# PE's order within a step of a language-model tower: the transposed scores behind the side product

## The chip, the cores and the metric

The kernel runs on one core of one Trainium2 chip. The metric is device time in microseconds (us), the median of several runs. Shown are three runs of the kernel before: 5783.61 us in the median, 5773.73 to 5789.76.

## The reference

One layer of a language model on 16 rows of 1024 token ids. Each row goes through three parts with residual sums between them, and a layer norm ahead of the second and the third:

- the **token part**: embedding rows are gathered, multiplied by a matrix, taken through six gated convolutions (width 3, 128 to 256 channels), and multiplied by a second matrix;
- the **attention**: eight heads of 16 channels, with two softmax maps each (from Wq1, Wk1 and Wq2, Wk2). Statistics of both maps over windows of four rows feed a small gate network, which mixes the two maps;
- the **experts**: layer norm, a matrix, then one of eight two-layer networks (128 to 512 to 128, gelu), a last matrix and a gelu.

```python
attn1 = jax.nn.softmax(jnp.einsum('bhqd,bhkd->bhqk', q1, k1) * scale, axis=-1)
attn2 = jax.nn.softmax(jnp.einsum('bhqd,bhkd->bhqk', q2, k2) * scale, axis=-1)
...
fused = alpha_full * attn1 + (1.0 - alpha_full) * attn2
out = jnp.einsum('bhqk,bhkd->bhqd', fused, v)
```

## The kernel before

The work on a row of tokens (a batch) is one long loop of 128 **steps**: 16 units (eight heads, two maps) of eight blocks of 128 query rows. Batches overlap: while the attention of batch i runs, the same steps carry the token part of batch i+1 (`PRE`) and the gates and experts of batch i-1 (`POST`). A planner (`plan`, lines 99 to 140, with costs and minimal distances) puts these side tasks into the steps, nearly always one that uses PE to a step, and leaves some steps without. The outer loop runs over two groups of eight batches, written out step by step.

A step n has four groups of work on PE (lines 397 to 439, 447 to 550):

- **scores**: two bf16 matmuls into `ps_s`, a buffer of two. DVE takes the negative and the row maximum from it into `neg_s` (L726), a step later the row minimum (L734);
- **weighted sum**: eight f32 matmuls of `exps` and the values into `ps_o`;
- **transposed scores** (`scores_t`): two bf16 matmuls into `ps_t`, which is a single buffer. They wait until the exp of the step before has read it. The maxima lie in three extra rows of the operand `qst`, so that the maximum is subtracted by the matmul itself;
- the **side product**, if there is one, into the bank `ps_w`, a single buffer too: three f32 matmuls for a half of a convolution on a quarter of the row (`conva`, `convg`, 256 columns), four for `fc1`, and so on.

ACT has in each step, in this order (lines 694 to 701): the exp of `ps_t` into `exps` (L594), the read of the side product out of `ps_w` (`va` and `ug` for the halves of a convolution, `hpre` for fc1), and the squares, a second exp of `neg_s` that sums up (L587). DVE has the row maximum, the row minimum, and the reads of those products that fall to it (the gate network, `wo`, `next`, `h2e`, `v`). POOL does the gating behind a convolution, the layer norms' arithmetic, the splitting of q and k into bf16 parts. SP loads the next unit's operands once enough transposed scores are done (line 375).

Each engine works through its instructions in the order written out, and waits on semaphores. The waits that matter here:

- `scores_t` of step n waits for the exp of step n-1 (line 414), and in the first block of a unit for the row of maxima (line 413);
- a side product waits until the product before it has been read out of the bank (`wait_bank`, lines 288 to 297), and for its own operands;
- the exp of step n waits for the transposed scores of step n (line 593), the read of a product for that product (line 610).

In one step, 80, ACT does all four gelus of the first expert layer ahead of its squares, and PE's `("fc2", 0)` waits for them one by one (line 505). `fc2p` and `("fc2", 1)` in steps 81 to 84 form one product spread over four steps.

Of the kernel before, what the change touches and what calls it, by code (L numbers as in the profile page):

```python
# [143 lines left out]
STEP = plan()  # L144
# [21 lines left out]
def tower_kernel(nc, ids, table, consts, w_e2h, b_e2h, conv_w, conv_b, w_h2e, b_h2e, wq1, wk1, wq2, wk2, wv, wo,  # L166
# [4 lines left out]
    with ExitStack() as ctx:  # L171
# [221 lines left out]
        def _(pe):  # L393
            def mm(dst, lhs, rhs, start=True, stop=True, **kw):
                return nc.tensor.matmul(dst, lhs, rhs, start=start, stop=stop, **kw)  # L395

            def scores(i, n):

                u, t = n // T, n % T
                if t == 0:  # L400
                    pe.wait_ge(s_ring[u % RING], i * (4 * 12 * 16) + 12 * 16 * (u // RING + 1))
                pe.wait_ge(s_max, i * STEPS + n + 1)
                for c in range(2):
                    last = mm(ps_s[:, n % 2, 512 * c:512 * c + 512], qst[0:KSC, u % RING, P * t:P * t + P],
                              kst[0:KSC, u % RING, 512 * c:512 * c + 512])
                last.then_inc(s_scores, 1)

            def scores_t(i, n):

                m = (n - LAG_T) % STEPS  # L410
                u, t = m // T, m % T
                if t == 0:
                    pe.wait_ge(s_mrow, i * (U * 64) + 64 * (n // T + 2))
                pe.wait_ge(s_exp, i * STEPS + n + 1)
                for c in range(2):
                    last = mm(ps_t[:, c, :], kst[:, u % RING, P * t:P * t + P],
                              qst[:, u % RING, 512 * c:512 * c + 512])
                last.then_inc(s_st, 1)

            def weighted(i, n, count=True, phase="body"):  # L420

                m = (n - LAG_V) % STEPS
                h, t = m // T % H, m % T
                if count:
                    pe.wait_ge(s_exp, i * STEPS + max(n, 1))
                    if t == 0:
                        wait_side(pe, phase, i, "dve", ("unit", n // T))
                    if m == 0:
                        wait_side(pe, "body", i, "pool", ("vcopy", 0))
                    if m == 6 * T:  # L430
                        wait_side(pe, "body", i, "pool", ("vcopy", 1))


                blocks = exps[:, (n - 2) % RING, :].rearrange("p (t q c) -> p q t c", t=T, q=4)
                for q in range(4):
                    last = mm(ps_o[32 * q:32 * q + 32, 0:QC], v_cur[:, t, VW * h:VW * h + 32],
                              blocks[:, q], start=(t == 0), stop=(t == T - 1))
                if count:
                    last.then_inc(s_pv, 1)
# [120 lines left out]
            with pe.Fori(0, NB // E) as group:  # L560
                for e in range(E):
                    i = group * E + e
                    for n in range(STEPS):
                        scores(i, n)
                        weighted(i, n)
                        scores_t(i, n)
                        for tk in STEP[n]:
                            task("body", i, tk)
            for n in range(LAG_V):
                if n < LAG_T:  # L570
                    scores_t(NB, n)
                weighted(NB, n, phase="tail")
# [5 lines left out]
        def _(act):  # L578
# [24 lines left out]
            def task(phase, i, tk):  # L603
# [26 lines left out]
                elif kind == "attw":  # L630
                    last = ident_act(xa[:, CH * tk[1]:CH * tk[1] + CH], bank[:, 0:CH], bias=col[:, 1:2])
                elif kind == "fc1":
                    _, c, j = tk
                    if (c, j) == (0, 0):
                        act.wait_ge(s_exw, i * 64 + 64)
# [10 lines left out]
                elif kind == "gelu2":  # L646
                    w("dve", ("next", 1))
                    last = nc.scalar.activation(z[:, :, :], z[:, :, :], ACT.Gelu)
                elif kind == "embT":
                    last = copy(emb_t[:, 512 * tk[1]:512 * tk[1] + 512], bank[:, :])  # L650
                elif kind == "e2h":
                    if tk[1] == 0:
                        w("pool", None)
                    last = ident_act(xc[:, 0, 1 + 512 * tk[1]:513 + 512 * tk[1]], bank[:, :], bias=col[:, 0:1])
                elif kind in ("conva", "convg"):
                    _, l, c = tk
                    k = CONV.index(tk) // 2
                    if kind == "conva" and k >= 2:
                        w("pool", CONV[2 * (k - 2) + 1])
                    if kind == "conva":  # L660
                        last = ident_act(va[:, c % 2, :], bank[:, 0:CH], bias=cb[:, 2 * l:2 * l + 1])
                    else:
                        last = nc.scalar.activation(ug[:, c % 2, :], bank[:, CH:2 * CH], ACT.Tanh, scale=0.5,  # L663
                                                    bias=cb_half[:, 2 * l + 1:2 * l + 2])
                elif kind == "xnT":
                    last = copy(xn_t[:, 512 * tk[1]:512 * tk[1] + 512], bank[:, :])
                elif kind == "qk":
                    _, a, which, k = tk
                    at = QK[a].index(tk)
                    if at >= 2:  # L670
                        w("pool", QK[a][at - 2])
                    elif phase == "body":
                        w("pool", None)

                    last = ident_act(stage[:, k, :], bank[:, :], scale=0.5 if which == 0 else 1.0)
# [422 lines left out]
```

## Time and profile before

| | |
|---|---|
| median of three runs | 5783.61 us (5773.73 to 5789.76) |
| the profiled execution | 5777.35 us |
| its span | 5775.5 us |
| busy: PE, ACT, DVE, POOL | 90%, 90%, 88%, 42% of the span |
| steps | 128 a batch, 16 batches |

The profile is of one execution. The span reaches from its first instruction to its last. An engine's line is what it was busy; "PE" are the matmuls, "PEld" the loads of weights that overlap them. In an answer in order of time a row gives the start, the duration, engine, line, operation, what is written from what, shapes and the number of instructions put together. In square brackets stands how long the engine had been idle before, and who released it. "L395" is a helper that all matmuls go through, so the tile's name tells which group it is.

### The profile page before, as it was taken

How to read it: one execution, taken by the hardware profiler on the slowest of the kernel's cores; microseconds unless marked ns; L12 is line 12 of the kernel's file. 1: busy time of each engine (PE TensorE's matmuls, PEld its weight loads, DVE VectorE, ACT ScalarE, POOL GpSimd, SP SyncE). 2: the span in 40 equal slices, each digit the busy share in tenths (PEclk: the TensorE clock that was granted, in tenths of full speed). 3: DMA queues.
4: the chain of work that ended last, by engine and by line, in shares of the span. 5: the costliest groups of instructions: out<-in, count | busy, mean ns of one | idle time of the engine just before them, and what ended most of it. 6: DMA issues, size and time to landing. Idle time of an engine off the chain costs nothing.

```text
span 5775.5 us, 120393 instructions
## 1 busy us (share of the span) xinstructions
PE 5177.0 (90%) x33798; PEld 2429.7 (42%) x33798; DVE 5109.5 (88%) x7715; ACT 5196.2 (90%) x7903; POOL 2454.1 (42%) x4439
## 2 busy tenths in 40 slices
PE   6998989899898998989889898998989899898995
PEld 4443434344343443434334343443434344343442
DVE  1989899898999989899898999989899898989983
ACT  2999999999999999999989999999999999999994
POOL 6525344352533525344352534525344352534523
PEclk8999999999999999999999999999999999999997
DMA  1001010010101001010010101001010010101000
GB/s 35 23 20 31 20 32 20 22 28 19 31 20 32 19 19 32 18 32 21 22 29 21 31 19 31 20 19 32 18 32 21 22 28 21 32 19 30 21 22 14
DMA packets 164931, 140.83 MB, mean 24 GB/s; under 512 B 89196, under 2 KB 108268, under 8 KB 164140
## 3 DMA queue, kind: packets, MB, share of 16 engines
q1 hardware_dynamic: 159100, 124.09, 9.3%
q0 software_dynamic: 4352, 8.92, 0.7%
q8 instruction: 289, 4.73, 0.3%
q14 instruction: 374, 3.06, 0.2%
q10 hardware_dynamic: 816, 0.02, 0.0%
HBM read 21.26 MB, written 8.91 MB: 5 GB/s over the span
## 4 chain that ended last, share of the span: by engine, by line
PE 41%; ACT 21%; issue 17%; POOL 10%; DVE 8%; SPq 2%; DMA 1%; ACTq 1%; POOLq 1%; DVEq 0%
PE ps_w L395 18%; PE ps_t L395 9%; ACT junk L587 9%; PE ps_o L395 7%; ACT exps L594 6%; PE ps_s L395 6%; DVE neg_s L726 3%; ACT hpre L598 2%; SPq L336 2%; DVE rowmin L734 1%; DVE bn L746 1%; POOL part L881 1%; POOL ctmp L1013 1%; POOL part L1015 1%; ACT stage L598 1%
## 5 line engine op out<-in xcount | busy, mean ns | idle before, releaser
L726 DVE TENSOR_SCALAR_CACHE_REDUCE neg_s<-ps_s 128x1024 f32<-128x1024 f32 x2048 | 2492.4, 1217 | 389.8 <-PE ps_s L395 338.3
L734 DVE TENSOR_REDUCE rowmin<-neg_s 128x1 f32<-128x1024 f32 x2049 | 2479.4, 1210 | 0.0
L587 ACT ACTIVATE junk<-neg_s,negmax 128x1024 bf16<-128x1024 f32 x2048 | 2357.9, 1151 | 112.8 <-DVE neg_s L726 106.4
L594 ACT ACTIVATE exps<-ps_t 128x1024 f32<-128x1024 f32 x2060 | 2116.0, 1027 | 179.7 <-PE ps_t L395 174.6
L395 PE MATMUL ps_t<-qst,kst 99*128 99x512 bf16 x4120 | 1274.4, 392 | 235.8 <-ACT exps L594 232.7
L395 PE MATMUL ps_o<-exps,v_cur 128*32 128x256 f32 x16512 | 1351.2, 400 | 143.8 <-DVE o_raw L742 120.8
L395 PE MATMUL ps_s<-kst,qst 96*128 96x512 bf16 x4096 | 1255.3, 388 | 67.3 <-DMA kst<-part 59.0
L395 PE MATMUL ps_w<-xc,cw 128*128 128x256 f32 x4704 | 1158.0, 382 | 3.7 <-DVE z L799 2.7
L395 PEld LDWEIGHTS ps_w<-xc,cw 128*128 128x128 f32 x4704 | 888.8, 190 | 221.2 <-DVE z L799 10.6
L395 PEld LDWEIGHTS ps_o<-exps,v_cur 128*32 128x32 f32 x16512 | 329.0, 109 | 1055.5 <-issue 643.0
L881 POOL TENSOR_SCALAR ctmp<-ug 128x256 f32<-128x256 f32 x408 | 165.8, 406 | 1331.4 <-ACT ug L663 1312.1
L395 PEld LDWEIGHTS ps_t<-qst,kst 99*128 99x128 bf16 x4120 | 236.4, 97 | 1148.1 <-issue 595.7
L395 PEld LDWEIGHTS ps_s<-kst,qst 96*128 96x128 bf16 x4096 | 397.0, 100 | 507.6 <-issue 198.1
L881 POOL TENSOR_SCALAR mparts<-negmax 128x8 bf16<-128x8 f32 x256 | 52.2, 204 | 866.0 <-DVE neg_s L726 826.4
L587 ACT ACTIVATION_READ_ACCUMULATOR junk<-neg_s,negmax 128x1 f32 x2048 | 412.1, 201 | 0.0
L1001 POOL TENSOR_TENSOR ctmp<-ctmp,va 128x256 f32<-128x256 f32 x408 | 298.0, 730 | 33.9
L1002 POOL TENSOR_TENSOR ctmp<-ctmp,xc 128x256 f32<-128x256 f32 x408 | 279.4, 685 | 32.0
L663 ACT ACTIVATE ug<-ps_w,cb_half 128x256 f32<-128x256 f32 x392 | 186.9, 477 | 65.1 <-PE ps_w L395 64.4
L598 ACT ACTIVATE va<-ps_w,cb 128x256 f32<-128x256 f32 x392 | 185.7, 474 | 63.6 <-PE ps_w L395 46.7
L395 PE MATMUL ps_w<-hpre,fc2s 128*128 128x512 f32 x264 | 163.6, 745 | 62.5 <-ACT hpre L643 62.5
L881 POOL TENSOR_SCALAR xc<-ctmp 128x256 f32<-128x256 f32 x408 | 167.6, 411 | 67.0 <-POOL ctmp L1002 67.0
L726 DVE DVE_READ_ACCUMULATOR neg_s<-ps_s 128x1 f32 x2048 | 170.2, 83 | 0.0
(181 smaller groups left out, 3932.8 us busy)
## 6 DMA issues: line engine op xcount, KB each, us to landing
qst<-part SPq DMA_DIRECT2D x1542, 32.0 KB, 2.0
kst<-part SPq DMA_DIRECT2D x1542, 32.0 KB, 2.0
qst<-mrow SPq DMA_DIRECT2D x1028, 1.5 KB
out_dram<-z SPq DMA_DIRECT2D x17, 512.0 KB, 3.2
fc1s<-in_fc_w SPq DMA_DIRECT2D x17, 256.0 KB
fc2s<-in_fc_w SPq DMA_DIRECT2D x17, 256.0 KB
cw<-in_conv_w SPq DMA_DIRECT2D x1, 2304.0 KB
odif<-in_table,idx POOLq DMA_INDIRECT x136
```

The lines of the kernel that those rows point to most:

```text
L336: sp.dma_start(dst[HD * g:HD * g + HD, r, :], part[HD * h:HD * h + HD, a, w, c, :])\
L395: return nc.tensor.matmul(dst, lhs, rhs, start=start, stop=stop, **kw)
L587: nc.scalar.activation(junk[:, n % 2, :], neg_s[:, n % SLOTS_S, :], ACT.Exp, scale=-1.0, bias=negmax[:, r, t:t + 1], accum_out=sumsq[:, r, ...
L594: nc.scalar.activation(exps[:, n % RING, :], ps_t[:, :, :].rearrange("p c q -> p (c q)"), ACT.Exp, scale=0.5).then_inc(s_exp, 1)
L598: return nc.scalar.activation(dst, src, ACT.Identity, **kw)
L663: last = nc.scalar.activation(ug[:, c % 2, :], bank[:, CH:2 * CH], ACT.Tanh, scale=0.5, bias=cb_half[:, 2 * l + 1:2 * l + 2])
L726: nc.vector.tensor_scalar(neg_s[:, n % SLOTS_S, :], ps_s[:, n % 2, :], -1.0, None, ALU.mult, ALU.min, accum_out=negmax[:, r, t:t + 1]).the ...
L734: nc.vector.tensor_reduce(rowmin[:, r, t:t + 1], neg_s[:, m % SLOTS_S, :], axis=AX, op=ALU.max, negate=True).then_inc(s_min, 1)
L746: last = nc.vector.bn_stats(bn[:, t, :], src[:, t, :])
L881: return nc.gpsimd.tensor_scalar(*args)
L1001: chain(i, tt(ctmp[:, 1, :], ctmp[:, 0, :], va[:, c % 2, :], ALU.mult))
L1002: chain(i, tt(ctmp[:, 2, :], ctmp[:, 1, :], x_in, ALU.add))
```

## The change

On PE, within a step of the main loop, the transposed scores are put behind the step's side tasks. Before they stood third, behind scores and weighted sum and ahead of the side product. Step 80, which holds `("fc2", 0)`, keeps the old order. Nothing else is touched: the prologue and the steps behind the main loop (lines 569 to 574), and the other engines' orders, stay.

```diff
                     for n in range(STEPS):
                         scores(i, n)
                         weighted(i, n)
-                        scores_t(i, n)
+                        if ("fc2", 0) in STEP[n]:
+                            scores_t(i, n)
                         for tk in STEP[n]:
                             task("body", i, tk)
+                        if ("fc2", 0) not in STEP[n]:
+                            scores_t(i, n)
```

## Rows read from the trace of the kernel before

**Rows 1.** The page: the span, and the engines' busy time.

```profile
span 5775.5 us, 120393 instructions
...
PE 5177.0 (90%) x33798; PEld 2429.7 (42%) x33798; DVE 5109.5 (88%) x7715; ACT 5196.2 (90%) x7903; POOL 2454.1 (42%) x4439
```

**Rows 2.** In order of time, PE and ACT: steps 66 (conv) and 67 (fc1).

```profile
2382.89 0.60 PE L395 MATMUL ps_t<-qst,kst 99*128 99x512 bf16 x2
...
2383.34 1.46 PE L395 MATMUL ps_w<-xc,cw 128*128 128x256 f32 x6
...
2384.63 0.60 PE L395 MATMUL ps_s<-kst,qst 96*128 96x512 bf16 x2
...
2384.91 0.47 ACT L598 ACTIVATE va<-ps_w,cb 128x256 f32<-128x256 f32 x1
...
2385.73 0.60 PE L395 MATMUL ps_t<-qst,kst 99*128 99x512 bf16 x2
...
2386.17 1.03 PE L395 MATMUL ps_w<-xa,fc1s 128*128 128x256 f32 x4
...
2386.43 1.02 ACT L594 ACTIVATE exps<-ps_t 128x1024 f32<-128x1024 f32 x1
...
2387.04 0.60 PE L395 MATMUL ps_s<-kst,qst 96*128 96x512 bf16 x2
...
2387.35 0.83 ACT L598 ACTIVATE hpre<-ps_w,fc1bs 128x256 f32<-128x256 f32 x2
```

**Rows 3.** The waits: engine, line, released by; us in total, times, longest.

```profile
PEld ps_t L395 <- ACT exps L594: 552.4, 741, 2.0
...
ACT ug L663 <- PE ps_w L395: 64.4, 238, 1.3
```

**Rows 4.** In order of time: a conv that waited for DVE's read (step 88).

```profile
2447.40 0.68 DVE L799 TENSOR_TENSOR z<-ps_w,row 128x512 f32<-128x512 f32 x1
...
2448.13 1.16 PEld L395 LDWEIGHTS ps_w<-xc,cw 128*128 128x128 f32 x6 [0.66 <-DVE z L799]
2448.14 1.56 PE L395 MATMUL ps_w<-xc,cw 128*128 128x256 f32 x6 [0.17 <-DVE z L799]
...
2449.53 0.60 PE L395 MATMUL ps_s<-kst,qst 96*128 96x512 bf16 x2
```

**Rows 5.** In order of time: fc2's first half is read, then step 81.

```profile
2429.61 0.69 ACT L598 ACTIVATE chan<-ps_w,fc2bs 128x512 f32<-128x512 f32 x1 [0.16 <-PE ps_w L395]
...
2430.51 0.60 PE L395 MATMUL ps_t<-qst,kst 99*128 99x512 bf16 x2
...
2431.21 1.02 ACT L594 ACTIVATE exps<-ps_t 128x1024 f32<-128x1024 f32 x1 [0.91 <-PE ps_t L395]
```

**Rows 6.** Exps alone, by stretches: us, ACT busy (number), PEclk, DMA share, GB/s.

```profile
2219.20:2234.37 15.17, 6.44 (x6) 1.00 0.05 12
2239.02:2247.39 8.37, 3.19 (x3) 1.00 0.05 12
2252.04:2259.92 7.88, 3.04 (x3) 1.00 0.21 46
2265.18:2312.17 46.99, 18.44 (x18) 1.00 0.08 19
2321.37:2336.23 14.86, 5.09 (x5) 0.89 0.08 17
2342.20:2417.88 75.68, 29.76 (x29) 1.00 0.10 22
2443.06:2486.90 43.84, 17.37 (x17) 1.00 0.09 20
```

**Rows 7.** In order of time: ACT's squares in step 42.

```profile
2320.23 1.15 ACT L587 ACTIVATE junk<-neg_s,negmax 128x1024 bf16<-128x1024 f32 x1 [2.40 <-DVE neg_s L726]
```

**Rows 8.** All engines, two stretches: PE, PEld, DVE, ACT, POOL, PEclk, DMA, GB/s.

```profile
2515.00:2530.00 15.00, 12.73 (x92) 4.25 (x90) 15.00 (x22) 15.00 (x24) 5.67 (x8) 1.00 0.12 28
2506.00:2514.00 8.00, 8.00 (x37) 1.80 (x36) 6.77 (x11) 6.40 (x10) 6.54 (x9) 0.51 0.14 42
```

## The prediction

> **What bounds the kernel now.** I read the page first: no engine is idle much, PE and ACT are both at 90% and DVE at 88% of a span of 5775.5 us [rows 1]. An average like this says only that three engines take turns, so the next view was one step of the dense part in order of time [rows 2]. There PE is the engine without a gap. From one group of transposed scores (ps_t) to the next lie 2385.73 - 2382.89 = 2.84 us, of which the conv product takes 2384.63 - 2383.34 = 1.29 and scores, weighted sum and transposed scores the other 1.55. With an fc1 product (2387.04 - 2386.17 = 0.87) it is 2.42. ACT needs less: from an exp to the read of the side product 2387.35 - 2386.43 = 0.92, from the read of a conv half to the next exp 2386.43 - 2384.91 = 1.52, in all 2.44. So a dense step now costs what PE's four groups cost, and the order on PE matters only if it makes PE stand.
>
> The waits say why it does not stand now [rows 3]: transposed scores wait for the exp before them (ps_t is one buffer), 552.4 us in all over 2048 steps, and ACT waits for a side product only 64.4 us at its largest group. ACT has squares and the read of the product to do while PE makes the next transposed scores, and PE has the side product to do while the exp runs. Each wait has cover.
>
> **The change, part by part.** Nothing is added or removed; in every step but 80 the transposed scores go behind the side product. Steps without a product keep their order.
>
> What moves on PE: two matmuls with their wait for the exp (and, every eighth step, for the row of maxima). They pass the product's matmuls and, which matters more, the product's waits: for the bank ps_w to be read by the step before, for POOL's conv output, for the expert's weights. The transposed scores issue no DMA. SP counts them before it loads the next unit, but that load is wanted some twelve steps later by the code; I cost it at nothing, with those steps as cover.
>
> *The new loop.* The product of step n waits until ACT has read the product of step n-1 out of ps_w. ACT does that read behind exp n-1. Exp n waits for the transposed scores n, and these now stand behind product n. So exp n-1, read n-1, product n, transposed scores n, exp n become one chain in which no two parts overlap. Its pieces:
> - exp to read: 0.92 [rows 2].
> - the read: 0.47 for a conv half, 0.83 for the two of fc1 [rows 2].
> - release of PE: DVE's read of ps_w ends at 2447.40 + 0.68 = 2448.08 and the waiting conv starts at 2448.14 [rows 4]: 0.06.
> - the product, started out of a wait: 2449.53 - 2448.14 = 1.39 for conv [rows 4], 0.10 more than without a wait, since its weights are loaded only behind the wait; fc1 by the same 0.10: 0.97.
> - transposed scores to exp, where ACT stands waiting: 2431.21 - 2430.51 = 0.70 [rows 5].
>
> The prices of a step behind a step whose product ACT reads: conv behind a conv (or another 256-wide read) 0.92 + 0.47 + 0.06 + 1.39 + 0.70 = 3.54 us, where PE's work is 2.84; fc1 (or attw, wo, a gate matmul, all taken as fc1) behind a conv 3.12; conv behind fc1 (or another wide read) 3.90; q/k and e2h behind one another 3.30, between 3.12 and 3.48 by the read; four transposes or the small alpha product 2.75 (an estimate: half the columns of fc1). Behind a product that DVE reads nothing waits for ACT, and PE's own 2.84 or 2.42 stands. A step without a product behind one with it falls to ACT's 2.44. A conv behind a step without a product: the transposed scores of that step start at the end of the exp before, 1.02 + 0.06 behind its start, then 1.55 + 1.29 + 0.70, in all 4.62 over two steps, less 2.44: 2.18.
>
> The Trainium skill bears on the 0.10: TensorE: Matmul & The Clock Gate, "Step-by-step: what each phase is for", lets PE pull weight loads ahead of running matmuls. By that rule a product would start with its weights in place, and the sum below would be some 90 us less; rows 4 disagree, as the load there begins at 2448.13, behind the wait, so the trace decides.
>
> *The sum over a batch.* The 128 steps of one batch from the middle, by stretches of steps with products, each row from exp to exp [rows 6]:
> - steps 5 to 11 (6): 2 x 2.75 + 4 x 3.30 = 18.7 for 15.17: +3.5.
> - 13 to 16 (3): 2 x 3.54 + 2.44 = 9.5 for 8.37: +1.2; 18 to 21 the same for 7.88: +1.6.
> - 22 to 40 (18): 4 x 3.54 + 5 x 3.12 + 3.90 + 3 x 2.75 + 4 x 2.84 + 2.42 = 55.7 for 46.99: +8.7.
> - 43 to 48 (5): 4 x 3.54 + 2.44 = 16.6 for 14.86: +1.7.
> - 50 to 79 (29): 7 x 3.54 + 12 x 3.12 + 8 x 3.90 + 2 x 2.75 = 98.9 for 75.68: +23.2. This is half of it: conv and fc1 or attw in turn, in every step.
> - 86 to 103 (17): 2 x 3.3 (next, read late by DVE, an estimate) + 2 x 3.54 + 4 x 2.44 + 4 x 2.18 + 4 x 3.54 + 3.12 = 49.4 for 43.84: +5.6.
> - step 81: fc2's first half is read from 2429.61 for 0.69 [rows 5]; then 0.06 + 0.97 + 0.70 puts exp 81 at 2432.03 instead of 2431.21: +0.8.
> - the steps at 41 and 104, which end a run: they no longer carry the product of the step before, 2.84 less 2.44 each: -0.8.
>
> Together 45.5. Against it stands that an ACT held up by PE lets DVE get ahead, and what DVE then has in hand covers part of its layer norm work, which now stops ACT for 2.40 [rows 7] behind ln2 and no longer than that behind ln3: between 0 and 4.8, the half, 2.4. Net 43.1, times 16 batches 690 us. The prologue and the tail are not touched. Against the profiled execution's 5777.35 us that gives 6467, and the runs' median is 6 us above it: I say 6470.
>
> *Bounds.* With every weight load ahead of its wait, the 56 pairs that are no transposes lose 0.10 each: -90 us; with the stops wholly covered another -38: 6340. With nothing covered +38, with DVE's reads late by 0.5 at its five places +40, with 0.05 more for each of 56 releases +45: 6590.
>
> **The rivals.**
>
> *Faster.* The standing of transposed scores for the exp, 552.4 us [rows 3], is filled by the product that now comes first, and ACT no longer waits for a conv half (64.4 us for the second half). This holds if the bank is free by then, that is, if ACT reads product n-1 ahead of exp n-1; from that point on the product costs nothing on the chain. For it: a step behind an empty one does run so. Against it: ACT's order has the exp first in every step, and rows 2 show the read 0.92 behind the exp's start. The price would be 5777 - 64 = 5713, at the very most 5777 - 552 = 5225.
>
> *No change.* PE's four groups are the same work in another order; if they bound all dense steps, 2.84 stays 2.84 and the time is 5777. It would need a bank that is free when PE comes to the product. Only a fifth of the steps with a product follow one without.
>
> *Slower by less.* The chain holds, but its parts overlap more than the rows show, or the stops give most of it back: half of 45.5 or less, below 5777 + 364 = 6140.
>
> *Slower by far more.* PE would stand 0.5 to 0.9 us in each dense step, and its clock could fall. In this trace the clock was 0.51 from 2506 to 2514, behind a stop, and 1.00 from 2515 to 2530, where PE was busy 12.73 of 15 us in gaps between short steps [rows 8]. In the chain PE would be busy 2.84 of 3.54, a little less. At 1.2 GHz a product of 1.39 and the transposed scores of 0.60 take twice that, +2.0 a pair, at 56 pairs and 16 batches 1790 us on top: 8260. If only some stretches fell, between. The Trainium skill, TensorE: Matmul & The Clock Gate, "A second HAM failure mode: psum-queue depth-cycling", tells of a kernel whose small standstills between matmul groups made the clock swing between its levels; by that rule the dense stretches here would be the place. The row of 2515 to 2530 does not agree with it at 85% busy.
>
> *The diff does less than it says.* Step 80 alone keeps the old order, since fc2 there waits for the gelu behind the exp; all other products are moved. This has no weight.
>
> **How the numbers follow.** The forecast 0.84, slower by less 0.07, slower by far more 0.04, no change 0.02, faster 0.03. Within the forecast the bounds give 6340 to 6590; a little more on each side, 6330 to 6600, leaves the other cases, about 0.16, outside. About 0.3% is what a measurement of this kernel can tell from no change: faster 0.03, same 0.02, slower 0.95.
>
> **What would show it.** In the profile after: exps to exps of 3.5 where conv follows conv and 7.0 for a pair of conv and fc1 (now 5.26); a new large wait of the exp for ps_t, some 0.8 to 1.2 us in each dense step, and of PE's ps_w for ACT's reads (va, ug, hpre); ACT's waits for ps_w gone; and DVE waiting longer for scores. PE's busy share falls to some 80%, while its clock stays at 1.00 in steps 50 to 79. I am wrong if exp follows exp at 2.84 in the dense part, if the wait of the exp is small, or if the clock is low there.

## The result, and the profile after

The changed kernel takes **6597.34 us** (median of 4 runs, 6594.74 to 6607.35), the kernel before beside it 5785.60 (4 runs). The ratio is 1.1409, 95% interval 1.139 to 1.1427: slower by 14%, some 812 us. The profiled execution took 6607.35 us. Forecast were 690 us more.

The page, against [rows 1]: as many instructions (120393) in a longer span (6605.5 us).

```profile
PE 5404.0 (82%) x33798; PEld 2490.5 (38%) x33798; DVE 5140.3 (78%) x7715; ACT 5198.9 (79%) x7903; POOL 2445.1 (37%) x4439
```

No engine is busy for more than 82% of the span now. ACT is busy for as long as it was, DVE within 31 us. PE is busy for 227 us more with the same 33798 matmuls (a conv group out of a wait counts 1.56 where it counted 1.46, and some groups ran at a lower clock; both below). The profile counts each f32 matmul of the code as two, so a conv half, three in the code, is x6, and the weighted sum, four in the code, is x8. What grew is waiting. The waits (engine, what it is about to do, released by: us in total, times, longest), of the kernel before:

```profile
ACT exps L594 <- PE ps_t L395: 174.6, 281, 19.9
```

and of the changed kernel:

```profile
ACT exps L597 <- PE ps_t L395: 1173.1, 1320, 19.9
DVE neg_s L729 <- PE ps_s L395: 1010.5, 888, 20.0
...
PE ps_w L395 <- ACT va L601: 233.2, 320, 3.6
```

The exp now waits 1173.1 us for the transposed scores, where it waited 174.6. PE stands (is idle) for ACT's read of the bank: 233.2 us for `va` alone, a wait that the kernel before does not have. The wait that the change makes shorter is that of PE's weight loads (PEld) for the exp, ahead of transposed scores: 552.4 in [rows 3], now 382.9. ACT's wait for the second conv half, 64.4 in [rows 3], is at 2.8.

One dense step in order of time, from exp 65 (fc1) over exp 66 (conv) to exp 67, against [rows 2]:

```profile
2729.66 1.02 ACT L597 ACTIVATE exps<-ps_t 128x1024 f32<-128x1024 f32 x1 [0.74 <-PE ps_t L395]
...
2730.58 0.83 ACT L601 ACTIVATE hpre<-ps_w,fc1bs 128x256 f32<-128x256 f32 x2
...
2731.47 1.56 PE L395 MATMUL ps_w<-xc,cw 128*128 128x256 f32 x6 [0.90 <-ACT hpre L601]
...
2732.86 0.60 PE L395 MATMUL ps_t<-qst,kst 99*128 99x512 bf16 x2
...
2733.56 1.02 ACT L597 ACTIVATE exps<-ps_t 128x1024 f32<-128x1024 f32 x1 [1.02 <-PE ps_t L395]
...
2734.48 0.47 ACT L601 ACTIVATE va<-ps_w,cb 128x256 f32<-128x256 f32 x1
...
2735.00 1.13 PE L395 MATMUL ps_w<-xa,fc1s 128*128 128x256 f32 x4 [0.54 <-ACT va L601]
2735.97 0.60 PE L395 MATMUL ps_t<-qst,kst 99*128 99x512 bf16 x2
2736.66 1.02 ACT L597 ACTIVATE exps<-ps_t 128x1024 f32<-128x1024 f32 x1 [0.59 <-PE ps_t L395]
```

It is the chain of the forecast, link by link: exp to read 0.92, the read 0.83 or 0.47, release 0.05 to 0.06, product 1.39 or 0.97, transposed scores to exp 0.70 or 0.69. Exp to exp is 2733.56 - 2729.66 = 3.90 for the conv behind fc1 (forecast 3.90) and 3.10 for fc1 behind the conv (3.12). The pair takes 7.00 where it took 5.26.

The exps by the same stretches of a middle batch as in [rows 6] (us, ACT busy, PEclk, DMA share, GB/s). PEclk is the granted clock of TensorE, as a mean over the stretch: 1.00 is 2.4 GHz, 0.50 is 1.2 GHz. Steps 5 to 11, 13 to 16, 18 to 21, 22 to 40, 43 to 48, 50 to 79, 86 to 103.

```profile
2535.14:2553.70 18.56, 6.15 (x7) 1.00 0.09 20
2558.48:2567.96 9.48, 3.07 (x3) 1.00 0.00 0
2572.67:2582.15 9.48, 3.07 (x4) 1.00 0.19 42
2587.41:2648.36 60.95, 18.41 (x18) 0.92 0.06 14
2656.21:2674.43 18.22, 5.10 (x5) 0.91 0.06 14
2679.53:2778.89 99.36, 29.67 (x29) 1.00 0.08 17
2806.45:2856.08 49.63, 17.40 (x17) 1.00 0.08 17
```

The forecast for these was 18.7, 9.5, 9.5, 55.7, 16.6, 98.9 and 49.4. Five of seven are within 0.5 us. Two are longer than forecast, by 5.3 and 1.6, and these are the two in which the clock column is not 1.00. So the experiments have two questions: is the chain the cause of the bulk, and is the clock the cause of what the forecast lacks?

Where a text below speaks of a mean by step, it is from the start of one exp to the next, over batches 2 to 15 of the profiled execution; where it says in how many of 14 batches something happened, it is these. By that count a batch went from 345.5 to 396.7 us: +51.2, against 43.1 forecast.

### The profile page after: what moved, and what is told of

It reads as the page before. It is cut to its first block, busy times and chain, and to the rows that moved or that the text cites. A ratio compares the mean times of both kernels' runs of the same rounds, so it can differ in the third digit from the quotient of the medians.

```text
span 6605.5 us, 120393 instructions
## 1 busy us (share of the span) xinstructions
PE 5404.0 (82%) x33798; PEld 2490.5 (38%) x33798; DVE 5140.3 (78%) x7715; ACT 5198.9 (79%) x7903; POOL 2445.1 (37%) x4439
## 4 chain that ended last, share of the span: by engine, by line
PE 43%; issue 23%; ACT 17%; POOL 7%; DVE 6%; ACTq 2%; SPq 1%; DMA 1%; POOLq 1%; DVEq 0%
PE ps_w L395 26%; PE ps_t L395 11%; ACT exps L597 4%; PE ps_o L395 3%; ACT junk L590 3%; PE ps_s L395 2%; ACT va L601 2%; ACT ug L666 2%; DVE neg_s L729 2%; ACT hpre L601 2%; SPq L336 1%; DVE rowmin L737 1%; DVE bn L749 1%; PE ps_w L444 1%; POOL part L884 1%
## 5 line engine op out<-in xcount | busy, mean ns | idle before, releaser
L729 DVE TENSOR_SCALAR_CACHE_REDUCE neg_s<-ps_s 128x1024 f32<-128x1024 f32 x2048 | 2495.8, 1219 | 1148.8 <-PE ps_s L395 1010.5
L597 ACT ACTIVATE exps<-ps_t 128x1024 f32<-128x1024 f32 x2060 | 2106.9, 1023 | 1185.0 <-PE ps_t L395 1173.1
L590 ACT ACTIVATE junk<-neg_s,negmax 128x1024 bf16<-128x1024 f32 x2048 | 2351.0, 1148 | 50.4 <-DVE neg_s L729 49.4
L395 PE MATMUL ps_w<-xc,cw 128*128 128x256 f32 x4704 | 1263.6, 405 | 367.0 <-ACT va L601 116.3
L395 PEld LDWEIGHTS ps_w<-xc,cw 128*128 128x128 f32 x4704 | 853.1, 194 | 824.5 <-ACT va L601 208.8
L395 PEld LDWEIGHTS ps_t<-qst,kst 99*128 99x128 bf16 x4120 | 353.6, 99 | 703.4 <-ACT exps L597 382.9
L395 PE MATMUL ps_w<-xa,fc1s 128*128 128x256 f32 x524 | 147.3, 404 | 71.7 <-ACT ug L666 37.3
```

The lines of the kernel that those rows point to most:

```text
L590: nc.scalar.activation(junk[:, n % 2, :], neg_s[:, n % SLOTS_S, :], ACT.Exp, scale=-1.0, bias=negmax[:, r, t:t + 1], accum_out=sumsq[:, r, ...
L597: nc.scalar.activation(exps[:, n % RING, :], ps_t[:, :, :].rearrange("p c q -> p (c q)"), ACT.Exp, scale=0.5).then_inc(s_exp, 1)
L729: nc.vector.tensor_scalar(neg_s[:, n % SLOTS_S, :], ps_s[:, n % 2, :], -1.0, None, ALU.mult, ALU.min, accum_out=negmax[:, r, t:t + 1]).the ...
```

## The experiments

**1. The old order back in the densest stretch.** The changed kernel, with the transposed scores third in steps 50 to 79.

```diff
-                        if ("fc2", 0) in STEP[n]:
+                        if n == 80 or 50 <= n < 80:
                             scores_t(i, n)
                         for tk in STEP[n]:
                             task("body", i, tk)
-                        if ("fc2", 0) not in STEP[n]:
+                        if not (n == 80 or 50 <= n < 80):
                             scores_t(i, n)
```

> The changed kernel, with the old order (transposed scores ahead of the side product) in steps 50 to 79 alone. Chain theory (exp, ACT's read of the product, the next product, the next transposed scores, the next exp run one behind the other wherever the step before has a product that ACT reads): this stretch alone takes back what the traces show for it, 75.7 in place of 99.4 us a batch, 23.7 x 16 = 379 us: 6597 - 379 = 6218 us. Rival, that the loss lies in the stops and in PE's clock behind them: the stretch has neither, so the time stays above 6550. Rival, that every step with a moved product loses the same: 29 of 96 such steps, 812 x 0.3 = 245 us: 6350.

Measured: 6213.03 us, ratio 1.0742 (1.0725 to 1.0758). That is 384 us off the changed kernel, 24.0 a batch, from 30 of the 128 steps. The exps of steps 50 to 79 in the same form as above:

```profile
2524.91:2600.59 75.68, 29.75 (x29) 1.00 0.10 22
```

75.68 is to the hundredth what the stretch took before [rows 6]. The loss is made in the step where the order stands, and ends with it. Both rivals, 6550 or more and 6350, are out.

**2. The new order only behind steps without a product.** The kernel before, with the transposed scores behind the product in 18 steps, those that carry a product on PE behind a step that carries none; there the bank is free.

```diff
-                        scores_t(i, n)
+                        if n not in BEHIND_EMPTY:
+                            scores_t(i, n)
                         for tk in STEP[n]:
                             task("body", i, tk)
+                        if not (n not in BEHIND_EMPTY):
+                            scores_t(i, n)
```

> The kernel before, with the new order only in the 18 steps whose step before has no product on PE, so that the bank is free when PE comes to the product. Chain theory: no chain arises, PE's work is the same, and a product made early takes the place of one made late: 5786 us within 0.6%, and no wait of the exp over 0.3 us in these steps. Rival, that the product of 0.9 to 1.3 us in front of the transposed scores is itself what delays the exp, bank or no bank: 18 x 0.9 x 16 = 260 us more, 6045.

Measured: 5805.10 us, ratio 1.004 (1.0026 to 1.0053), 19 us over the kernel before. The order by itself costs next to nothing. One part of the expectation missed: the exp waited for more than 0.3 us in seven of the 18 steps (22, 86, 92, 95, 98, 101 and 118, by 0.4 to 1.3). Those from 86 to 101 are made up again in the steps behind them: from exp 85 to exp 113 a batch takes as long as in the kernel before. The 19 us show in two places: from exp 21 to exp 22 (+0.99 in the mean) and from 117 to 118 (+1.13). There the weighted sum waits until DVE has taken the unit's old output out of `ps_o` (into `o_raw`; "the collect" below), and the product comes behind that.

**3. The same without the steps of the collect** (22, 86 and 118).

```diff
-BEHIND_EMPTY = [n for n in range(1, STEPS) if on_pe(n) and not on_pe(n - 1)]
+BEHIND_EMPTY = [n for n in range(1, STEPS) if on_pe(n) and not on_pe(n - 1) and n % T != LAG_V % T]
```

> The kernel with the new order only behind empty steps (5805 us), now without steps 22, 86 and 118, in which the weighted sum waits until DVE has collected the unit's sums. If its extra 19 us come from the product standing behind that wait and the transposed scores behind the product: these three steps take back 1.0, 0.5 and 1.1 us a batch, 36 to 42 us less: 5763 to 5770, a little under the kernel before. Rival, that the extra is the product behind the weighted sum in all 18 steps: 5800.

Measured: 5786.45 us, ratio 1.0005 (0.9996 to 1.0013), between the two theories. The 19 us are gone, but nothing is gained: the steps that got shorter by 0.4 (18 to 21) and 0.8 (13 to 16) are paid back in step 44 (+0.6, with the clock down in 11 of 14 batches where it was down in 6) and elsewhere. Now step 22 in order of time, first in experiment 2 (product ahead of the transposed scores):

```profile
2272.62 0.64 PE L400 MATMUL ps_o<-exps,v_cur 128*32 128x256 f32 x8 [1.89 <-DVE o_raw L750]
2273.19 2.93 PE L400 MATMUL ps_w<-xc,cw 128*128 128x256 f32 x6
```

and in experiment 3 (old order there):

```profile
2269.33 0.64 PE L400 MATMUL ps_o<-exps,v_cur 128*32 128x256 f32 x8 [1.88 <-DVE o_raw L750]
...
2270.34 1.46 PE L400 MATMUL ps_w<-xc,cw 128*128 128x256 f32 x6
```

The same conv takes 2.93 in the one and 1.46 in the other. The windows behind the stand (PE, PEld, DVE, ACT, POOL, PEclk, DMA share, GB/s) say why, of experiment 2 and then of experiment 3:

```profile
2272.60:2276.90 4.30, 4.28 (x18) 2.53 (x18) 3.34 (x4) 3.11 (x6) 3.57 (x7) 0.60 0.00 0
```

```profile
2269.30:2273.40 4.10, 3.48 (x26) 1.76 (x26) 4.10 (x5) 4.06 (x8) 3.38 (x7) 1.00 0.00 0
```

0.60 against 1.00: PE ran mostly at 1.2 GHz in the one and at 2.4 in the other. This is no fixed difference between the two programs: behind this stand the clock fell in 12 of 14 batches of experiment 2 and in 3 of 14 of experiment 3. What tells the batches apart stays open.

The two places differ. From exp 21 to exp 22 the price is the clock's: in the two batches of experiment 2 in which the clock held, the step took 5.26 us, as in the kernel before. From 117 to 118 the clock stood at 1.00 in every batch of both experiments, and the step took 3.49 in each against 2.53 in experiment 3: there the product behind the collect costs by itself.

**4. The old order in 22 and 118 of the changed kernel.**

```diff
-                        if ("fc2", 0) in STEP[n]:
+                        if n in (22, 80, 118):
                             scores_t(i, n)
                         for tk in STEP[n]:
                             task("body", i, tk)
-                        if ("fc2", 0) not in STEP[n]:
+                        if n not in (22, 80, 118):
                             scores_t(i, n)
```

> The changed kernel, with the old place of the transposed scores in two steps of each batch, 22 and 118. In both the weighted sum stands on PE until DVE has collected the old output, and with the new order the side product comes behind that wait and ahead of the transposed scores. Theory (a product behind the collect is a cost of its own, which the forecast did not have): 117 to 118 lose the 1.3 us that they have over the kernel before, 22 loses 1.0 to 1.4, the clock's share at 23 stays; -2.3 to -2.7 us a batch, -37 to -43 in all, less up to 0.9 a batch taken back at the end of the batch: 6555 to 6575 us. Rival (what is lost there is the clock's, or stands on DVE and comes back within a step): under 0.5 us a batch, 6590 to 6600 us.

Measured: 6585.30 us (6568.07 to 6591.87), ratio 1.1369 (1.1347 to 1.1392). 12 us, between the two theories; its interval just touches that of the changed kernel. By step it is -0.42 at 22, -0.89 at 117, but +0.37 at 118 and +0.34 at 119, and the batch ends 0.66 shorter. The collect is a small cost, not the 8 us a batch that the forecast lacks. In the changed kernel step 117 lasts from 2.04 to 4.84 us by batch, in this one from 2.03 to 3.41. Two effects are mixed in that. In batches with a clock of 1.00 there, the step takes 2.92 in the mean of the changed kernel (8 of 14) and 2.03 here (5 of 14), so the old order saves 0.9. But the clock fell in 6 of 14 batches there and in 9 here, and behind a fall the steps 118 and 119 are longer here. In such a batch of the changed kernel, behind a stand of 1.21 us for the collect, the two q/k matmuls (into `ps_w` from `xn_t`) took 2.01 us; in a batch whose clock stands at 1.00 they take 1.13.

**5. Idle matmuls where PE stands.** The changed kernel, with f32 matmuls of 256 columns into an unused half of `ps_o`, which nothing reads: 7 in step 23, 1 in 30, 3 in 44, 9 in 80, ahead of the side product.

```diff
+            def spin(k):
+                for _ in range(k):
+                    mm(ps_o[:, QC:512], cw[:, 0, 0, 0:P], cw[:, 0, 1, 0:CH], start=False, stop=False,
+                       skip_group_check=True)
...
+                        spin({23: 7, 30: 1, 44: 3, 80: 9}.get(n, 0))
                         for tk in STEP[n]:
                             task("body", i, tk)
```

> The changed kernel, with extra f32 matmuls of 256 columns on PE whose result nobody reads, where PE stands long: 7 in step 23 ahead of the first gate product, 1 in step 30, 3 in step 44, 9 in step 80 ahead of fc2. They only add work. Clock theory (what the forecast missed, 8 us a batch, is products at half the clock behind these stands: steps 23 to 24, 30, 44 and 80): the clock stays up there, step 23 to 24 falls from 5.8 to about 3, and the time falls by up to 126 us, to 6470 to 6520. Rival, that those steps wait for operands (DVE's read of the gate product, POOL's conv output) and the low clock only goes with it: no gain, 6597 or up to 90 us more for the added work.

Measured: 6533.24 us, ratio 1.1292 (1.1274 to 1.1309): 64 us faster than the changed kernel, with more work in it. Steps 23 and 24 of the changed kernel in order of time:

```profile
2588.91 1.33 PE L395 MATMUL ps_w<-cst,gin 128*64 128x32 f32 x16 [3.56 <-ACT va L601]
...
2593.00 2.93 PE L395 MATMUL ps_w<-xc,cw 128*128 128x256 f32 x6
```

and of experiment 5:

```profile
2558.99 1.11 PE L395 MATMUL ps_w<-cst,gin 128*64 128x32 f32 x16 [0.33 <-ACT va L607]
...
2561.58 1.56 PE L395 MATMUL ps_w<-xc,cw 128*128 128x256 f32 x6
```

The conv is back from 2.93 to 1.56. The transposed scores ahead of it, not shown, went from 1.03 to 0.61. The windows from exp 22 to exp 24, of the changed kernel and of experiment 5 (columns as above):

```profile
2587.41:2597.06 9.65, 8.15 (x40) 4.25 (x40) 2.90 (x5) 4.65 (x9) 0.81 (x5) 0.65 0.01 3
```

```profile
2557.50:2563.95 6.45, 6.12 (x46) 3.62 (x45) 2.90 (x5) 4.64 (x9) 0.81 (x5) 1.00 0.01 4
```

In the mean by step: 22 and 23 are shorter by 2.88, 29 by 0.70, 43 by 0.65, 80 by 0.90: 5.1 us a batch, of which step 127 takes 0.86 back. The clock is shown to cost time in the changed kernel. How much of that the change brought is another question: the kernel before too loses to the clock at 44 and 80 (below and experiment 10), so the 0.65 and the 0.90 say little on that. The expected range, 6470 to 6520, was missed: the saving of up to 126 us was taken from one batch, and other batches lose less.

**6. ACT reads the product first.** The changed kernel, and on ACT the read of the side product moved ahead of the exp, in every step but 80. The orders of PE and ACT match again.

```diff
+                        for tk in STEP[n]:
+                            if "pe" in ENGINES[tk[0]] and ("fc2", 0) not in STEP[n]:
+                                task("body", i, tk)
                         exp_t(i, n)
                         for tk in STEP[n]:
-                            if tk != ("fc2", 0):
+                            if "pe" not in ENGINES[tk[0]]:
                                 task("body", i, tk)
```

> The changed kernel, with ACT's order changed to match: in every step but 80 ACT reads the side product out of the bank ahead of the exp, not behind it. Chain theory: the read no longer stands behind the exp, so the next product no longer waits for it; PE is back to its own 2.84 us for a conv step and 2.42 for an fc1 step, and the time is that of the kernel before, 5720 to 5850 us. Rival, that the order on PE is itself the cost (transposed scores come 1.3 us later behind the exp than before): it stays near 6600.

Measured: 5841.06 us, ratio 1.0096 (1.008 to 1.0111). With PE's new order untouched, 756 of the 812 us are gone. The exps of steps 50 to 79:

```profile
2367.91:2446.18 78.27, 29.73 (x29) 1.00 0.10 21
```

Not quite 75.68: a conv step takes 2.93 where it was 2.84, although PE waits for nobody. Step 68 in order of time:

```profile
2412.91 0.83 ACT L601 ACTIVATE hpre<-ps_w,fc1bs 128x256 f32<-128x256 f32 x2
...
2413.62 0.64 PE L395 MATMUL ps_o<-exps,v_cur 128*32 128x256 f32 x8
...
2414.19 1.16 PEld L395 LDWEIGHTS ps_w<-xc,cw 128*128 128x128 f32 x6 [0.41 <-ACT hpre L601]
2414.19 1.56 PE L395 MATMUL ps_w<-xc,cw 128*128 128x256 f32 x6
2415.59 0.60 PE L395 MATMUL ps_t<-qst,kst 99*128 99x512 bf16 x2
```

The conv's row names no idle time: PE was busy with the weighted sum until the conv began. The row of the load names ACT's read as what released it, but that read was done at 2412.91 + 0.83 = 2413.74, 0.45 earlier. Yet the conv's first weights are loaded at its own start, and it takes 2415.59 - 2414.19 = 1.40, the price that the prediction gave to a product behind a wait.

**7. The mirror.** The kernel before (PE's old order) with ACT's read ahead of the exp: the same edit on ACT as in experiment 6.

> The kernel before with PE's order left alone, but ACT reads the side product ahead of the exp in every step but 80 (the other half of the change that brought the time back). Chain theory: the mirror of the slow kernel. The exp now waits for the product, which stands behind the transposed scores, which wait for the exp before: 0.44 from transposed scores to product, 1.46 for a conv, 0.1 to ACT, 0.38 for the read, 1.02 for the exp, 0.06 back to PE, some 3.4 us for every conv step, also behind an empty step, and about 3.3 for fc1: 48 conv steps at +0.75, 8 of fc1 at +0.6, some 16 others at +0.5, 48 us a batch, 6450 to 6650 us. Rival, that an exp made later costs nothing as long as PE has work: 5786.

Measured: 6539.69 us, ratio 1.1307 (1.1291 to 1.1324). The other mismatch costs nearly as much as the change. One of its steps in order of time:

```profile
2704.06 1.02 ACT L594 ACTIVATE exps<-ps_t 128x1024 f32<-128x1024 f32 x1
...
2705.23 0.59 PE L395 MATMUL ps_t<-qst,kst 99*128 99x512 bf16 x2 [0.93 <-ACT exps L594]
2705.66 1.46 PE L395 MATMUL ps_w<-xc,cw 128*128 128x256 f32 x6
...
2707.16 0.47 ACT L663 ACTIVATE ug<-ps_w,cb_half 128x256 f32<-128x256 f32 x1 [0.94 <-PE ps_w L395]
...
2707.53 1.02 ACT L594 ACTIVATE exps<-ps_t 128x1024 f32<-128x1024 f32 x1
```

The exp has its operand in good time, but stands on ACT behind the read of a product that PE makes only after the exp before. The chain is exp, transposed scores, product, read, exp: 3.47 us.

**8. Experiment 6 with the weighted sum ahead of the scores on PE**, so that the product follows the 512-column scores.

```diff
-                        scores(i, n)
                         weighted(i, n)
+                        scores(i, n)
```

> The kernel with the new order on PE and the read first on ACT (5841 us), with the weighted sum ahead of the scores, so that the side product follows the scores and not the eight narrow matmuls of the weighted sum. If the 0.09 us by which its conv steps are longer than PE's 2.84 (2.93) come from a full-width weight load that is not made ahead behind the narrow matmuls: 2.84 for a conv step, 2.42 for fc1, and 5841 - 16 x 3 = 5790 us, near the kernel before. Rival, that the 0.09 are the product's wait for its bank: no change, 5841.

Measured: 5951.00 us, ratio 1.0285 (1.0272 to 1.0298). Both theories missed the total by over 100 us. The steps show where: behind the collect the scores are now held up too (21 and 22 longer by 2.0, 109 by 0.9, 85 by 0.8, 5 by 0.5), and so at products that DVE reads (39 by 0.8, 32 by 0.7, 27 by 0.6). The part that was to be told did come: from an fc1 exp to the next conv exp fell from 2.66 to 2.48, with 2.76 from there to the next fc1 exp in both, so 0.09 a step. The product in order of time:

```profile
2462.85 1.27 PEld L395 LDWEIGHTS ps_w<-xc,cw 128*128 128x128 f32 x6
...
2463.07 1.46 PE L395 MATMUL ps_w<-xc,cw 128*128 128x256 f32 x6
2464.36 0.60 PE L395 MATMUL ps_t<-qst,kst 99*128 99x512 bf16 x2
```

Here the load begins 0.22 ahead of the product, beside the scores, and the conv takes 1.29.

**9. The changed kernel with the same swap**, so that the product both follows the scores and waits for ACT's read (the same edit, in the changed kernel).

> The changed kernel, with the weighted sum ahead of the scores on PE, so that a side product follows the 512-column scores and not the 32-column weighted sum; it waits for ACT's read of the bank as before. Theory 1 (the weights are loaded only behind the wait, whatever stands ahead): the conv group in the chain stays at 1.39 us and exp to exp at conv behind conv at 3.54. Theory 2 (the 0.10 comes from following the narrow matmuls alone): 1.29 and 3.44 us. The total does not tell them apart, as the weighted sum now holds the scores up where it waits for DVE's collect: by theory 1 6600 to 6720 us, by theory 2 6510 to 6630 us.

Measured: 6640.85 us, ratio 1.1476 (1.1457 to 1.1495). The total is in the range of theory 1, and so is the step:

```profile
2742.91 1.16 PEld L395 LDWEIGHTS ps_w<-xc,cw 128*128 128x128 f32 x6 [1.29 <-ACT hpre L601]
2742.91 1.56 PE L395 MATMUL ps_w<-xc,cw 128*128 128x256 f32 x6 [0.80 <-ACT hpre L601]
2744.31 0.60 PE L395 MATMUL ps_t<-qst,kst 99*128 99x512 bf16 x2
```

1.40 from conv to transposed scores, with the load at the moment of the product, although nothing narrow stands ahead. So a product has the 0.10 behind a wait with nothing narrow ahead (here), and behind the narrow matmuls of the weighted sum without a wait (experiment 6).

**10. Idle matmuls in the kernel before.** If stands cost clock in the changed kernel, they should in the kernel before: 5 ahead of step 0's scores, 9 in step 110 ahead of the weighted sum, 8 in step 80 ahead of fc2. Their results are read by nobody.

```diff
+                        if n == 0:
+                            spin(5)
                         scores(i, n)
+                        if n == 110:
+                            wait_side(pe, "body", i, "dve", ("h2e", 1))
+                            spin(9, ps_w[:, 0:CH])
                         weighted(i, n)
                         scores_t(i, n)
+                        if n == 80:
+                            spin(8)
```

> The kernel before with extra matmuls whose result nobody reads where PE stands long: 5 ahead of step 0, 9 in step 110 ahead of the weighted sum, 8 in step 80 ahead of fc2. Clock theory: behind these stands PE runs at half the clock (steps 109 to 112 take 9.9 us for 8.2 at the full clock); with the fill 2 us of that and 0.5 each at 80 and 0 come back, 3 us a batch, 48 us less: 5735 to 5750. Rival, that a stand costs its own length only and the clock behind it is hidden: 5786 or more.

Measured: 5756.85 us, ratio 0.9954 (0.9942 to 0.9965). This **beats both kernels**, by 26 us over the kernel before (5782.41 beside it), about half of the 48 that were expected, and outside the range: 80 is shorter by 1.73, 109 to 111 by 1.3, 44 by 0.56 (though nothing was put in there), 0 by 0.37, but 113 is longer by 1.1 and 81 by 0.5. From exp 80 to exp 81, the kernel before and then experiment 10 (columns as above):

```profile
2420.66:2431.21 10.55, 7.10 (x21) 2.84 (x22) 2.20 (x5) 9.42 (x12) 0.00 (x0) 0.84 0.12 26
```

```profile
2404.37:2413.63 9.26, 8.50 (x34) 3.94 (x32) 2.41 (x5) 9.20 (x12) 0.00 (x0) 1.00 0.11 24
```

Two products in turn in two halves of `ps_w`, which would take away the wait for the read itself, were not tried.

## Why the prediction was right in its chain, and the step that failed

**The chain: right.** Exp, read, release, product, transposed scores and exp follow one another without overlap, with the links forecast. Conv behind conv 3.53 (3.54), fc1 behind conv 3.10 (3.12), conv behind fc1 3.90 to 3.97 (3.90), q/k and e2h 3.22 to 3.31 (3.30), transposes 2.75 (2.75), conv behind an empty step 2.30 (2.18). Experiment 1 shows that the order makes the loss where it stands, 6 and 7 that it is the mismatch between PE's and ACT's orders: either engine alone in the other order costs 13 to 14%, both together 1%.

**What the order costs alone: nothing that can be told** (experiment 3), as the prediction had it by costing the matmuls themselves at nothing.

**The 0.10 of a product behind a wait: right in size**, and experiment 9 shows the wait to be a reason. It is not the only one: products without a wait pay it too, as they now follow the weighted sum (experiment 6). The prediction left it out there. It put 2.84 for a conv behind a product that DVE reads, measured 2.91 to 2.93 in steps 25, 27 and 32, and most of the 0.12 at the conv behind an empty step is this.

**The sum by stretches: this is the step that failed.** It lacked 8.1 us a batch, and three places make up nearly all of that.

*"22 to 40: +8.7" measured +13.2 in the mean.* The term is added up from prices at the full clock, and the change made PE's clock fall there. The kernel before held 1.00 over this stretch in every batch. In it PE comes to the place where ACT stops for `std` (two loads of tables of 1.28 us around the square roots, in step 21) in two stands, one for DVE's collect and one for the exp, with a weighted sum, transposed scores, a conv, scores and another weighted sum between them:

```profile
2261.84 0.64 PE L395 MATMUL ps_o<-exps,v_cur 128*32 128x256 f32 x8 [1.57 <-DVE o_raw L742]
...
2266.25 0.61 PE L395 MATMUL ps_t<-qst,kst 99*128 99x512 bf16 x2 [0.94 <-ACT exps L594]
```

In the changed kernel DVE had made the collect by the time that PE came to it, so the first stand is gone:

```profile
2581.78 0.64 PE L395 MATMUL ps_o<-exps,v_cur 128*32 128x256 f32 x8
```

And the transposed scores of step 23 may not go ahead of their product, which waits for ACT's read. So all of PE's work up to there is done early, and one stand of 3.56 is left (2588.91, experiment 5). The conv behind it took 2.93, on the chain. At step 30 the clock fell once more (4.70 from exp 29 to exp 30). With idle matmuls in the stands the stretch came back by 3.5 in the mean. In the 8 of 14 batches of experiment 5 in which its clock then stood at 1.00 it took 55.99 to 56.27, where the forecast was 55.7:

```profile
3343.79:3399.78 55.99, 18.39 (x18) 1.00 0.07 16
```

So the prices were right for the full clock, and the clock is what this term lacked.

*"43 to 48: +1.7" measured +3.4 in the mean.* Here the time after was priced rightly, and the row of the kernel before was not typical. The batch of [rows 6] took 14.86 at a clock of 0.89; in 6 of 14 batches a conv runs slowly there, in the other 8 the stretch takes 13.19. A batch of the kernel before and one of the changed kernel, both at the full clock:

```profile
2667.28:2680.47 13.19, 5.10 (x6) 1.00 0.08 18
```

```profile
3053.06:3069.73 16.67, 5.10 (x5) 1.00 0.06 14
```

That is +3.5, and 16.67 is the forecast's 16.6. In the changed kernel the clock falls here in 6 of 14 batches as well, and adds about as much (16.67 to some 18.2). So the sum set a price at the full clock against a row at a lower one.

*Steps 117 to 123 were in no term*: 117 and 118 +1.3, 119 to 122 +0.7. In 117 and 118 a q/k product stands behind the collect; in the 8 batches with the full clock the two take +0.6, so the rest, some 0.8 in the mean, goes with the clock, which fell there in 6 of 14 batches and in none of the kernel before (no run tests this alone). In step 122 a q/k product has another product behind it: 3.23 where it was 2.51, a price that the prediction had (3.30) and did not apply there.

The rest is small, beside what the terms had: +0.5 in steps 50 to 79, +0.2 in 86 to 103, +0.6 in all at 0 to 21 and 79 to 86, -0.2 in what comes back (below), and -1.2 at 123 to 127, which no term had.

**What comes back: right in its sum, with luck.** The ends of the runs were put at -0.8, and 40 and 103 gave -0.4 each. The stops of ACT behind ln2 and ln3 were put at -2.4, the half of a range that no row decided; they gave -0.8 (42) and -0.9 (49), and a third stop that was in no term gave -0.8 (107).

**The total: near, in part by luck.** 6597 is above the 6590 to which the bounds were added up from rows, and inside 6330 to 6600 by the 10 us that were put on top. The terms that were to bring it up to 6590 (stops not covered at all, DVE's reads late, slower releases) are not what brought it there.

**The rivals.** *Faster* and *no change* needed a bank that is free early. Experiment 6 makes it so and comes out 1% above the kernel before, so the condition was rightly named and rightly put aside. The 552.4 us in the price of *faster* are idle time of the weight loads; PE itself stood 232.7 us for the exp there. *Slower by less* is out. *Slower by far more, by the clock* was refused for the dense stretch, and rightly: from exp 50 to exp 79 the clock stood at 1.00, with PE standing 0.5 to 1.0 us in every step (all engines, PE first):

```profile
2679.53:2778.89 99.36, 79.56 (x502) 41.06 (x499) 72.28 (x97) 76.12 (x124) 26.34 (x58) 1.00 0.08 17
```

PE was busy for 79.56 of these 99.36 us. What the Trainium skill tells of a kernel whose standstills between matmul groups made the clock swing (TensorE: Matmul & The Clock Gate, "A second HAM failure mode: psum-queue depth-cycling") did not happen in this stretch. But that rival's sentence that some stretches might fall and give a time between is what happened: at the few longer stands of each batch, not in the dense part.

**The signs that it named** came, one of them in half: PE busy 82%, ACT's wait for ug down to 2.8, DVE's wait for scores 1010.5, and 7.00 for a pair. The exp's wait for the transposed scores was put at 0.8 to 1.2 in each dense step; it is 1.02 and 0.59 in turn.

## What to carry to other kernels

Where one engine fills two single buffers and another empties both, keep the orders on the two alike: here what PE makes first ACT has to read first. In both cases tried, a change of one order alone put the two buffers' handovers one behind another in one chain. The price of a step could be worked out beforehand from five rows of the trace. When summing it, look where the new order gathers short stands of PE into a long one, and price the groups behind it from a row at the lower clock: once they lie on the chain, nothing hides them. And look at several batches of the kernel before: a stretch that takes 13.19 in one and 14.87 in another is no basis by a single row.

## What the runs showed of the hardware that was not expected

- **A load of weights does not run ahead behind the weighted sum.** Behind its eight 32-column matmuls, the next group's first load began with the group, though nothing was left to wait for (2414.19, experiment 6); behind the 512-column scores it began 0.22 earlier (2462.85, experiment 8). The conv groups take 1.40 and 1.29. The Trainium skill (TensorE: Matmul & The Clock Gate, "Step-by-step: what each phase is for") has loads pulled ahead of matmuls in flight when their row groups do not conflict or the load goes to the background weight buffer. Experiment 8 agrees with a pull ahead; whether experiment 6 falls outside those conditions no run here shows. In experiment 9 the load began only behind the wait (2742.91), a case for which that sentence names no rule.
- **Idle matmuls buy time.** 20 of them a batch gave 64 us of 6597 (experiment 5), 22 a batch 26 us of 5782 (experiment 10); in the windows shown the granted clock was then 1.00 where it had been 0.65 and 0.84.
- **The same stand does not always cost clock.** After PE had stood 1.9 us for the same collect, the granted clock fell in 12 of 14 batches of one program and in 3 of 14 of another (0.60 and 1.00 in the two windows shown). What tells them apart is open.
